# Attention values of two heads on 32 shared rows, with their denominators beside them

## The reference

```python
x = x + jnp.tanh(g_xattn[0]) * _L0_xattn_ref(_layernorm(x, axis=-1), ctx_1024, ctx_1024, W, b, mask)
x = x + jnp.tanh(g_ffn[0]) * _L0_ffn_ref(_layernorm(x, axis=-1), ...)

# _L0_xattn_ref: 16 heads of 16, no projection of q, k, v
scores = jnp.einsum('bhqd,bhkd->bhqk', qh, kh) / jnp.sqrt(jnp.asarray(dh, q.dtype))
scores = jnp.where(merged == 1, NEG_INF, scores)      # causal, or the key is masked
attn = jax.nn.softmax(scores, axis=-1)
out = jnp.einsum('bhqk,bhkd->bhqd', attn, vh)
return out.transpose(0, 2, 1, 3).reshape(B, Sq, D) @ W.T + b
```

## Time and profile before

| | us |
|---|---|
| three executions | 1179.38, 1179.4, 1188.54 |
| profiled execution, its own time | 1187.3 |
| its span | 1185.6 |
| TensorE (PE) busy | 1111.3 (94%) |
| VectorE (DVE) busy | 811.3 (68%) |
| ScalarE (ACT) busy | 470.9 (40%) |
| GpSimd (POOL) busy | 520.4 (44%) |
| mean granted clock of TensorE | 0.969 |

### The profile page before, as it was taken

One profiled execution on the slowest core, in us unless ns is written; L12 is line 12 of the kernel. 1 busy time (PEld: TensorE's weight loads), 2 busy tenths in 40 slices (PEclk: granted clock), 3 DMA queues, 4 the chain that ended last, 5 costly groups with the idle time before them and its releaser, 6 DMA issues.

```text
span 1185.6 us, 22481 instructions
## 1 busy us (share of the span) xinstructions
PE 1111.3 (94%) x7475; PEld 924.6 (78%) x7475; DVE 811.3 (68%) x1778; ACT 470.9 (40%) x723; POOL 520.4 (44%) x647
## 2 busy tenths in 40 slices
PE   3779999999999999999999899999999899999997
PEld 2557877887887887887787677888888788888886
DVE  6466686676686686685786776547544488777876
ACT  4455555544554555555545442223322111121110
POOL 5233456356356447447357333300000466666664
PEclk8788999998999999999999999999999899999999
DMA  8977566657656657547554511468664455555552
GB/s 146 223 116 140 121 98 137 122 91 139 123 93 136 128 111 117 138 110 106 130 121 70 129 36 43 154 214 268 196 206 134 146 157 157 156 159 155 159 158 79
DMA packets 106163, 160.65 MB, mean 136 GB/s; under 512 B 28828, under 2 KB 70718, under 8 KB 106048
## 3 DMA queue, kind: packets, MB, share of 16 engines
q1 hardware_dynamic: 94276, 121.18, 45.8%
q0 software_dynamic: 11776, 38.03, 10.5%
HBM read 75.24 MB, written 52.10 MB: 107 GB/s over the span
## 4 chain that ended last, share of the span: by engine, by line
PE 68%; issue 10%; DVE 10%; POOL 8%; DMA 2%; ACT 1%; POOLq 0%; SPq 0%; DVEq 0%; ACTq 0%
PE ps L741 15%; PE ps L788 12%; PE ps L686 8%; PE ps L790 6%; PE ps L703 5%; POOL tab_dram L1452 3%; PE ps L594 3%; PE ps L773 3%; PE ps L637 3%; PE ps L606 3%; PE ps L562 2%; POOL regr L1403 2%; PE ps L566 1%; PE ps L615 1%; PE ps L660 1%
## 5 line engine op out<-in xcount | busy, mean ns | idle before, releaser
L788 PE MATMUL ps<-regr,gh 128*128 x600 | 222.0, 407 | 0.1
L870 ACT ACTIVATE Pt<-ps,pbias 77x1024 f32<-77x1024 f32 x128 | 141.4, 1105 | 165.9 <-PE ps L594 155.1
L790 PE MATMUL ps<-regr,gl 128*128 x600 | 170.1, 284 | 0.0
L788 PEld LDWEIGHTS ps<-regr,gh 128*128 128x128 f32 x600 | 114.0, 190 | 24.0 <-issue 0.7
L960 ACT ACTIVATE gh<-ps 128x512 fp32r<-128x512 f32 x75 | 44.4, 598 | 205.9 <-PE ps L773 115.9
L1170 DVE TENSOR_REDUCE mneg<-ps 128x8 f32<-128x616 f32 x128 | 101.3, 793 | 30.5 <-PE ps L566 30.4
L790 PEld LDWEIGHTS ps<-regr,gl 128*128 128x128 f32 x600 | 114.2, 190 | 0.0
L686 PE MATMUL ps<-x2h,winh 128*128 128x512 f32 x256 | 112.5, 439 | 0.6 <-DVE OHR L1075 0.6
L1353 POOL TENSOR_TENSOR gl<-gf,gh 128x512 fp32r<-128x512 f32 x64 | 82.3, 1287 | 61.5 <-ACT gh L827 61.1
L1428 POOL TENSOR_TENSOR x<-x,regf 128x512 f32<-128x512 f32 x32 | 41.1, 1286 | 150.7 <-DMA x<-in_x 150.7
L686 PE MATMUL ps<-x2h,winl 128*128 128x512 f32 x256 | 102.2, 399 | 0.0
(11 more groups left out here) (202 smaller groups left out, 2685.1 us busy)
## 6 DMA issues: line engine op xcount, KB each, us to landing
regr<-regr SPq DMA_DIRECT2D x96, 256.0 KB, 6.0
y_dram<-Pt SPq DMA_DIRECT2D x64, 256.0 KB, 2.2
regf<-in_x SPq DMA_DIRECT2D x32, 256.0 KB, 3.4
x<-in_x SPq DMA_DIRECT2D x32, 256.0 KB, 7.3
y_dram<-res SPq DMA_DIRECT2D x32, 256.0 KB
regr<-regr SPq DMA_DIRECT2D x96, 77.0 KB, 6.8
x_dram<-x2h SPq DMA_DIRECT2D x14, 512.0 KB, 3.0
x_dram<-x2l SPq DMA_DIRECT2D x14, 512.0 KB, 3.8
```

Source lines behind the costliest of these rows:

```text
L788: e.matmul(o, gh2[:, k % 3, fc, :], w2v[:, bass.ds(val, 1), fc, :, :].rearrange("p o h d -> p (o h) d"), start=fc == 0, stop=False, skip_g ...
L790: m = e.matmul(o[:, 0, :], gl2[:, k % 3, fc, :], w2v[:, bass.ds(val, 1), fc, 0, :].rearrange("p o d -> p (o d)"), start=False, stop=fc == ...
L870: e.activation(Pt[0:K, 4 * k:4 * k + 4, :].rearrange("k (n j) t -> k n (j t)", n=2), bank_of["sc", b, k][0:K, :, :], ACT.Exp, bias=pbias[: ...
```

## The change

1. `Vau` no longer has a column of ones. A head with an odd number has its 16 values in columns 16 to 31, one with an even number in 0 to 15, and the other half is zero. Two heads are summed into the same 32 rows, so 8 heads fill 128 partitions of half a bank. The other half gets the denominators, by the same matmuls with `vone` (ones in the one half of the columns) as weights: each head's denominator stands on all 16 rows beside its values.
2. What comes out is already turned and in the order that the projection needs. The stages `att` and `attT` go, with their 12 transposes, the two copies to `OT` and the bank of O. VectorE takes a reciprocal of 128 x 256 denominators and multiplies, twice for a sequence; a stage `halves` splits the result into `aTh` and `aTl`, from SBUF.
3. `xT` goes from slot 7 to slot 6, ahead of the last scores and of `norm2`.
4. `gates` goes from slot 3 to slot 10 of iteration 1; the masks of the later sequences wait on SP until the first maxima transfer has landed, and `load_x1` of sequence 0, with the big weights behind it, until the second has.

```diff
-                    (11, "load_x1", 0), (11, "att", 0)))
+                    (11, "load_x1", 0), (11, "halves", 0)))
...
-        put(i, ((2, "norm", 0), (7, "xT", 0), (10, "queries", 0)))
+        put(i, ((2, "norm", 0), (6, "xT", 0), (10, "queries", 0)))
...
-            slots[3].append(("gates", 0, 0))
-            slots[10].append(("zeros", 0, 0))
+            slots[10] += [("gates", 0, 0), ("zeros", 0, 0)]
...
-                "sc": lambda: (s["P"], 4 * n + k + 1), "val": lambda: (s["OT"], 2 * n + k + 1),
-                "O": lambda: (s["att"], n + 1), "aT": lambda: (s["aTl"], n + 1), "pj": lambda: (s["x1"], n + 1),
+                "sc": lambda: (s["P"], 4 * n + k + 1), "val": lambda: (s["att"], 2 * n + k + 1), "pj": lambda: (s["x1"], n + 1),
...
                 elif stage_ == "masks" and b == 1:
                     e.wait_ge(s["ks1"], 2)
+                    e.wait_ge(s["mt0"], 16)
...
                     if b == 0:
                         e.wait_ge(s["ks1"], 2)
+                        e.wait_ge(s["mt1"], 16)
...
                     for q in range(2):
-                        for j in range(4):
-                            n = 8 * k + 4 * q + j
-                            m = e.matmul(bk[32 * j:32 * j + 32, q * S:(q + 1) * S], Vau[:, ks, g, n, :], Pt[0:K, n, :],
-                                         start=True, stop=True)
+                        for odd in range(2):
+                            for j in range(4):
+                                n = 8 * k + 2 * j + odd
+                                m = e.matmul(bk[32 * j:32 * j + 32, q * S:(q + 1) * S], vone[:, odd, :] if q else Vau[:, ks, g, n, :],
+                                             Pt[0:K, n, :], start=odd == 0, stop=odd == 1)
...
-                elif stage_ == "values":
-                    e.wait_ge(s["val"], 2 * b + k + 1)
-                    if b >= 1 and k == 0:
-                        e.wait_ge(s["O"], b)
-                    e.activation(OT[:, 2 * k:2 * k + 2, :], bank_of["val", b, k][:, :].rearrange("p (q t) -> p q t", q=2),
-                                 ACT.Copy).then_inc(s["OT"], 1)
...
+                elif stage_ == "halves":
+                    e.wait_ge(s["att"], 2 * b + 2)
                     if b >= 1:
                         e.wait_ge(s["pj"], b)
+                    e.activation(aTh[:, :, :], att[:, :, :], ACT.Copy).then_inc(s["aTh"], 1)
...
+                elif stage_ == "values":
+                    v = bank_of["val", b, k]
+                    e.wait_ge(s["val"], 2 * b + k + 1)
+                    e.reciprocal(rdT[:, k, :], v[:, S:2 * S]).then_inc(s["rden"], 1)
+                    e.wait_ge(s["rden"], 2 * b + k + 1)
+                    e.tensor_tensor(att[:, k, :], v[:, 0:S], rdT[:, k, :], ALU.mult).then_inc(s["att"], 1)
+                elif stage_ == "halves":
+                    e.wait_ge(s["aTh"], b + 1)
...
+                    e.tensor_tensor(aTl[:, :, :], att[:, :, :], aTh[:, :, :].bitcast(F), ALU.subtract).then_inc(s["aTl"], 1)
```

More of the change, by code:

```diff
@@ L99, in phase_one @@
         put(i - 2, ((1, "scores", 0), (3, "scores", 1), (5, "scores", 2), (5, "values", 0), (7, "scores", 3), (8, "values", 1),
-                    (11, "load_x1", 0), (11, "att", 0)))
+                    (11, "load_x1", 0), (11, "halves", 0)))
         put(i - 1, ((0, "max", 0), (2, "max", 1), (4, "max", 2), (6, "max", 3), (9, "maxT", 0)))
-        put(i - 3, ((2, "bias", 0), (1, "attT", 0), (4, "proj", 0), (7, "norm2", 0), (10, "x2T", 0)) if i < NB + 2 else
-            ((1, "bias", 0), (1, "attT", 0), (3, "proj", 0), (5, "norm2", 0), (7, "x2T", 0), (9, "logits", 0), (10, "logitsT", 0)))
-        put(i, ((2, "norm", 0), (7, "xT", 0), (10, "queries", 0)))
+        put(i - 3, ((2, "bias", 0), (4, "proj", 0), (7, "norm2", 0), (10, "x2T", 0)) if i < NB + 2 else
+            ((1, "bias", 0), (3, "proj", 0), (5, "norm2", 0), (7, "x2T", 0), (9, "logits", 0), (10, "logitsT", 0)))
+        put(i, ((2, "norm", 0), (6, "xT", 0), (10, "queries", 0)))
         put(i + 1, ((8, "moments", 0),))
@@ L298, in build @@
         Vau = carve(K, [2, G, H, 32], regf)
-        OT = carve(P, [4, S], regf)
-        att = carve(P, [2, H, DH], regf)
+        rdT = carve(P, [2, S], regf)
+        att = carve(P, [2, S], regf)
         identb = sb("identb", [P, P], BF)
@@ L370, in build @@
         wt_s = xn2[:, :, :]
-        att_f = att[:, :, :, :].rearrange("p t h d -> p t (h d)")
         w1f = regf[:, w1_at:w1_at + 2048].rearrange("p (c k n) -> p c k n", c=2, k=2)
@@ L600, in tensor @@
                         e.wait_ge(s["vau"], b // G + 1)
+                    if b == 0 and k == 0:
+                        e.wait_ge(s["dcon"], DCON["va_one"])
                     e.wait_ge(sem, v)
```

54 lines of the change are left out of this document (13 added, 41 removed).

## The result

The changed kernel takes 1250.5 us (median of four executions, 1247.67 to 1258.04), the kernel before 1182.7 in the same comparison (1179.38 to 1188.54; a fourth execution, 1186.0, moved its median up from 1179.4): ratio 1.058, 95% interval 1.051 to 1.065. It is 68 us slower, where I had forecast 16. The profiled executions are 63.1 us apart (spans 1248.7 and 1185.6), and it is these 63.1 that the traces explain.

A forecast was written before the change was run, and what follows sets the result against it. TensorE was taken to bound the filled stretch, transfers and latency the start. Terms 15.7 + 16 - 4 - 5 - 1 - 6 = +15.7 us, put on the median 1179.4, gave 1195 us; range 1166 to 1217.

The forecast's parts named there:

- `xT` sooner, loads, with their clock: Shorter `xTl` stalls -4 us, half the lost clock back -5, earlier transfers at the start -6.
- `att`, `attT` and the bank of O away, a copy in place of the reciprocal: TensorE: 1.24 us of removed work in each of 28 sequences, and -1 us for the wait at O's bank.
- the denominators' matmuls: TensorE's two `values` stages: four more rounds each, 0.9 us a stage, +1.8 us a sequence, 28 sequences.
- the reciprocal, with the bank of `x2T`: `x2T` waits for VectorE's reciprocal and product to free its bank: 0.8 us on 20 sequences, +16 us (9 to 40).
- TensorE's work, net: Filled stretch: added rounds less removed transposes, +0.56 us a sequence, 28 sequences, +15.7 us (10 to 22).
- wait of `x2T`, less the waits for `xTl`, `norm2` and O: New bank wait at `x2T` +16 us, shorter stalls behind late `norm2` -4, O's bank wait gone -1.
- start: First sequences: maxima transfer 3 to 4 us shorter, a wait behind weight splittings gone; together -6 us (-14 to +3).
- its bounds: VectorE's reciprocal of 256 values from PSUM: 0.59 us at the lower end, 1.76 at the upper, 1.5 taken.
- Together 1.24 us for each sequence: TensorE: removed `att` transposes 0.79 us, `attT` transposes 0.36, and 0.09 from the fp32r matmul behind them.
- It stays below TensorE on average (17.9 of 20.7): VectorE's queue: with +2.7 us on 15.2 a sequence it remains less loaded than TensorE.
- rival (1): VectorE decides in routing iterations: half of 28 sequences pay 2.7 us at `x2T` or `proj`, 38 us, 1217; chance 0.15.
- Half of the lost clock: TensorE's filled stretch: of an estimated 10 us lost to lowered clock, half returns as stalls go, -5 us.

The follow-up runs named there:

- a_noden: The changed kernel without the denominators' matmuls (8 instead of 16 in each `values` stage), the reciprocal reading the values instead: 1228.7 us.
- b_all: The kernel before with everything of the change but the attention part (`xT` in slot 6, `gates` in slot 10, later masks and `load_x1`): 1171.2 us.
- a_neither: The changed kernel without the denominators' matmuls and with a plain copy of the values in place of the reciprocal: 1172.4 us.
- a_norecip: The changed kernel with the reciprocal replaced by a plain copy of the same size from PSUM: 1208.1 us.
- an_cover: The changed kernel without denominators' matmuls and reciprocal, with 8 more 128x128 transposes in every `x2T`: 1180.8 us.
- b_recip: The kernel before with an added 128x256 reciprocal from SBUF on VectorE at each `values` stage from the third sequence, nobody waiting for it: 1213.3 us.
- b_xt6: The kernel before with `xT` one slot sooner (slot 6) and nothing else changed: 1171.4 us.

## Why the prediction was wrong in size

The direction was right, and the wait that it named is the largest one; the sum was not: 15.7 us forecast, 67.8 measured. Four kernels split the way from the one to the other, each step by medians and uncertain by some 8 us; the steps depend on their order (the denominators alone were worth 22 us in a_noden):

| step | forecast | measured |
|---|---|---|
| `xT` sooner, loads, with their clock | -4 - 5 - 6 = -15 | -11.5 (b_all less before) |
| `att`, `attT` and the bank of O away, a copy in place of the reciprocal | 28 x -1.24 - 1 = -35.7 | +1.2 (a_neither less b_all) |
| the denominators' matmuls | 28 x 1.8 = +50.4 | +35.7 (a_norecip less a_neither) |
| the reciprocal, with the bank of `x2T` | +16 | +42.4 (changed less a_norecip) |
| sum | +15.7 | +67.8 |

The same by the terms of its sum, from the profiled executions, which are 63.1 apart:

| term | forecast | measured |
|---|---|---|
| TensorE's work, net | +15.7 | +18.1 (a_norecip less b_all) |
| wait of `x2T`, less the waits for `xTl`, `norm2` and O | +11 | +15.1 |
| wait for the row maxima | none | +14.0 |
| other idle time (the rest of the 33.0) | none | +3.9 |
| clock (the rest of the 21.3 of busy time) | -5 | +3.2 |
| start | -6 | +7.9 |
| behind sequence 31 | none | +0.8 |

**Right.** Four rounds more cost 0.86 us a stage (1.87 less 1.01; 0.82 by the two kernels with and without them; 0.9 taken). The removed transposes were worth 1.0 us a sequence, 0.24 less than I took from the timeline. The reciprocal was in its bounds, at the upper end, and a wait at `x2T` takes 1.1 us on average, where 0.8 was taken for 20 of them. TensorE waits for L1170 at `x2T` 27 times (20 to 30 forecast), the waits for `xTl` are down to 2.1 us in 5, none longer than 0.4, and the maxima transfer lands in 4.93 us instead of the 7.76 of the earlier trace rows:

```profile
39.70 4.93 DMA regr<-regr
```

**The step that failed first: removed work costed at its full length.** "Together 1.24 us for each sequence" counts `att` and `attT` as time on the path. It promised 35 us, and a_neither shows none: with 28.0 us of TensorE work less, 26.6 more are spent waiting. The transposes lay between `x2T` and the second `max`, beside the queue of VectorE that ends with the row maxima of the `max` before. The prediction asked what hides each added edit; it did not ask what the removed ones had hidden. They had hidden two things. TensorE's part covered some of VectorE's queue, as an_cover shows. VectorE's part kept the routing steps out of POOL's way: of the +14.0 at the maxima, 8.6 go when the collision goes. And the bank of `x2T` hangs on VectorE's product even without the reciprocal: 14.0 us of added waits in a_neither. No run takes away the transposes and nothing else.

**The second: VectorE's load was checked by its average.** "It stays below TensorE on average (17.9 of 20.7)" is true, and VectorE did get 2.8 us more for each sequence (515.9 and 436.7 over 28). But b_recip shows that 3.5 us for each sequence, with nobody waiting for them, cost 28 us there, and the reciprocal, priced at 16 us by the stall at one bank, cost 42. My rival (1) had this mechanism, at 38 us instead of 16 and chance 0.15; it was nearest to the result, but bound it to stalls at `x2T` or `proj`, and had neither the maxima nor the start in it. VectorE's busy share was forecast at 86 to 90 of 100 and came out at 80 to 81, since the sequences themselves became longer: a share that stays low is no proof that the engine isn't the cause.

**The third: the clock.** Half of the lost clock was to come back. It did come back where the stalls went (1.00 throughout in b_xt6), but the changed kernel has more stalls than before, and the granted clock over the 28 sequences is 0.97 (0.98 before).

**The fourth: the start.** The transfer got faster as forecast, and up to the first `x2T` nothing is lost (60.55 against 61.61). All of it comes between the `x2T` of sequences 0 and 3, 67.8 us long instead of 58.9. There TensorE's busy time grew by 8.6 us (57.9 from 49.4), its idle time by 0.4, and its granted clock is 0.76 instead of 0.88. So the three sequences cost more than their added work (3 x 0.56 us by the prediction's count) because they run at the lower clock for longer. The term took no account of what the attention part does there: sequence 3 is at 128.39 in the changed kernel, 124.23 without the reciprocal, 119.71 without the denominators, 117.95 with neither. Between 100 and 110 us the granted clock is 0.50 (the lower level, 1.2 GHz), where it was 0.90; from 60 to 130 us TensorE had waited 6.4 us for VectorE's product at `x2T` and 4.7 for ScalarE's exp at `values`:

```profile
100.00:110.00 10.00, 8.01 (x46) 4.95 (x46) 5.83 (x12) 2.01 (x6) 2.54 (x6) 0.50 0.36 53
```

What stays open: how the 8.7 us of start that the denominators cost and the 4.2 of the reciprocal, taken away one by one, split into work, waits and clock, where two executions of the same instructions can differ by 3 us; how the 26.6 us of a_neither split between TensorE's missing transposes and VectorE's moved work; and one wait of 4.5 us at its `x2T`. No run was made for these.

## What to carry to other kernels

Before work is taken off the bounding engine, look at what runs beside it: where another engine's queue ends just in time, much of the removed work comes back as waits, and it is worth the slack, not its length. Look also at what the removed instructions kept apart on the other engines. An engine that is idle a quarter of the time can still be the one that decides; price added work there by putting it into the old kernel with nobody waiting for it, and not by its average share. And test a wait by taking its cause away: 30 us of waits at one bank were worth 10 to 15, and a sooner transpose that gave 11 us in one kernel gave none in the other.
